# Attention scores of a transformer kernel issued at the pace of the next block's row maxima

## The chip, the cores and the metric

The kernel runs on one core of one Trainium2 chip. The metric is the device time of one execution in microseconds (us). The kernel before took 1959.16 us, the median of 3 runs (1953.23 to 1961.06). The profile comes from one further execution, which took 1958.59 us.

Five engines work side by side, each through its own instruction stream in order: PE (TensorE, matrix products; PEld is its weight load), DVE (VectorE), ACT (ScalarE), POOL (GpSimd) and SP (SyncE), which only issues DMAs here. They wait for one another with semaphores. PE writes to eight PSUM banks of 128 x 512 float32.

## The reference, cut to what matters

One sequence of 2048 tokens with 256 features passes four residual layers: attention with a linear position bias, a layer of 64 experts, attention with low-rank keys and values, and the experts again. The change touches both attention layers, which share one order of work. Per head (16 heads of 16 features), in the first:

```python
scores = jnp.einsum('bhqd,bhkd->bhqk', q, k)
scores = jnp.where(causal[None, None], scores, NEG)
scores = scores + bias[None]
scores = scores / jnp.sqrt(jnp.float32(D))
w = jax.nn.softmax(scores, axis=-1)
ctx = jnp.einsum('bhqk,bhkd->bqhd', w, v).reshape(b, s, e)
return ctx @ Wo + bo
```

The softmax subtracts each query's largest score, so that every score is computed twice: once to find the maxima, and once more, transposed, for the exponents.

## The kernel before

The core of an attention layer (the part between the projections and the experts) is cut into 16 **blocks**: 4 groups of 4 heads, and in each 4 blocks of 512 queries. `BLOCKS` runs through a group's blocks b = 0, 1, 2, 3, and in the last group through 3, 2, 1, 0. A block goes through two passes.

The **maxima** of a block: PE multiplies queries by keys into one of three PSUM banks (L1686; parts on the diagonal get a mask added by small products, L1692), and DVE reduces the bank to row maxima (L2146, L2152). One such product with its reduction is called a maximum here. Block b needs 16b + 10 of them: 10, 26, 42, 58. When the last is reduced, DVE combines them (L2162), PE transposes the result (the **turn**, L1700), DVE splits it in two parts (L2172, L2174), and SP sends them by DMA as extra rows of the query operand. Only then can the block's exponents start.

The **units** of a block: one for each 128 keys, 4(b + 1) of them, each with two scores items (two products each, L1714, on 52 of the rows, into the two `exp_banks`), two exponents on ACT (L1346) and one product of the exponents with the values (L1728, "pv" in the code, called the value product here), which accumulates in one bank over the block. In the last four units of a block the causal mask shortens the rows: 512, 384, 256, 128. After the last value product ACT copies the bank out (L1355), PE transposes it (`ctx`, L1740), and ACT, DVE and POOL finish the context.

While the units of one block run, PE also issues the maxima of the next block. Both share PE's one stream, and the order in it is fixed before the kernel is built: `core_plan()` (L134) keeps four streams, contexts, maxima, scores and value products, and estimated finishing times of the engines. It repeatedly takes the item that can start earliest by those estimates (`ready`), the maxima winning ties over the scores. The turn of a block stands in the maxima's stream behind the first two maxima of the next block (`items.insert(2, ...)`). All engines walk through the same resulting list. `NP` = 3 is the number of buffers for exponents: unit e may not be scored before the value product of unit e - 3.

## Time and profile before

| | us | share of the span |
|---|---|---|
| profiled execution, its own time | 1958.59 | |
| span, first to last instruction | 1956.8 | 100% |
| PE busy | 1677.0 | 86% |
| DVE busy | 1426.4 | 73% |
| ACT busy | 1127.2 | 58% |
| POOL busy | 698.0 | 36% |

The span holds everything but 1.8 us of the execution's time. The two attention cores lie at about 60 to 526 us and 1027 to 1492 us, some 466 us each; the experts fill most of the rest. Busy time adds up what an engine's records cover, so an engine can be busy without being at its peak. PEclk is the TensorE clock that was granted: 1.0 is 2.4 GHz and 0.5 is 1.2 GHz.

### The profile page before, as it was taken

The page shows a single profiled execution, that of the slowest core. Times are in us where ns is not written, and L with a number is a line of the kernel's source. Part 1 is how long each engine was busy: PE and PEld are TensorE (multiplying, and loading weights), DVE is VectorE, ACT ScalarE, POOL GpSimd, SP SyncE. Part 2 cuts the span into 40 slices and gives each one's busy share as a digit, 9 for nine tenths or more (in the row PEclk, how much of TensorE's full clock was granted, in tenths as well). Part 3 has the DMA queues.
Part 4 walks back from the last instruction along what each step waited for, and adds up shares of the span by engine and source line. Part 5 has one row for each costly group of instructions (what it writes and reads, how often), then busy time and mean ns, then how long its engine had stood idle before and what let it go on. Part 6 is the DMA issues. An engine that isn't in the chain of part 4 may idle for free.

```text
span 1956.8 us, 36378 instructions
## 1 busy us (share of the span) xinstructions
PE 1677.0 (86%) x12410; PEld 1037.7 (53%) x12410; DVE 1426.4 (73%) x3057; ACT 1127.2 (58%) x1999; POOL 698.0 (36%) x788
## 2 busy tenths in 40 slices
PE   6899999999977789987788999999999787889910
PEld 5545444445556677775334454544446566777710
DVE  5688888888487765886548788888866788558843
ACT  2155757667557677664233457576664676777610
POOL 6000101000257556545660001010012674754466
PEclk9677989889989999999897779898899899999955
DMA  6540120300075556665854104030003555666643
GB/s 234 174 70 2 30 40 12 57 2 2 23 275 170 178 173 199 203 197 181 250 168 86 20 2 62 6 53 14 2 7 105 217 175 170 204 195 203 202 140 118
DMA packets 127906, 225.96 MB, mean 115 GB/s; under 512 B 15364, under 2 KB 91028, under 8 KB 123444
## 3 DMA queue, kind: packets, MB, share of 16 engines
q1 hardware_dynamic: 103152, 156.49, 26.4%
q0 software_dynamic: 24576, 67.14, 12.7%
q8 instruction: 106, 1.74, 0.4%
q14 instruction: 72, 0.59, 0.1%
HBM read 124.20 MB, written 98.84 MB: 114 GB/s over the span
## 4 chain that ended last, share of the span: by engine, by line
PE 58%; DVE 13%; DMA 9%; issue 8%; POOL 7%; ACT 3%; SPq 1%; DVEq 0%; ACTq 0%; POOLq 0%
PE late_banks L1728 14%; PE late_banks L1686 12%; PE exp_banks L1714 8%; PE late_banks L1517 7%; PE exp_banks L1534 6%; POOL ring_t L1093 4%; DMA ring_t<-token_rows,index_t 3%; DVE chunk_max_t L2146 3%; POOL ring_t L1088 3%; DVE inter_t L2027 3%; PE late_banks L1550 2%; DMA ring_t<-expert_rows,rows_of_t 2%; DMA expert_rows<-outs_t 2%; PE late_banks L1492 2%; PE late_banks L1692 2%
## 5 line engine op out<-in xcount | busy, mean ns | idle before, releaser
L1346 ACT ACTIVATE probs_t<-exp_banks 128x1024 f32<-128x1024 f32 (+3 forms) x640 | 538.9, 896 | 291.7 <-PE exp_banks L1714 289.0
L2146 DVE TENSOR_REDUCE chunk_max_t<-late_banks 128x1 f32<-128x512 f32 (+1 forms) x960 | 602.5, 682 | 111.7 <-PE late_banks L1686 87.4
L1184 POOL TENSOR_SCALAR_AFFINE_SELECT probs_t<-probs_t 128x512 f32<-128x512 f32 x128 | 81.3, 635 | 676.7 <-ACT probs_t L1346 676.7
L1728 PE MATMUL late_banks<-probs_t,values_t 128*32 128x512 f32 (+3 forms) x2560 | 318.7, 572 | 1.9 <-POOL probs_t L1184 1.1
L1093 POOL DMA_INDIRECT ring_t<-expert_rows,rows_of_t x256 | 243.9, 953 | 189.3 <-DVE x_sb_t L2045 127.4
L1517 PE MATMUL late_banks<-tokensT_t,fetched_t 128*128 x2048 | 299.2, 291 | 10.9 <-issue 5.6
L1088 POOL DMA_INDIRECT ring_t<-token_rows,index_t x256 | 251.3, 982 | 139.2 <-PE late_banks L1492 78.5
L2027 DVE TENSOR_TENSOR inter_t<-late_banks,silu_t 64x256 f32<-64x256 f32 x512 | 217.5, 425 | 91.0 <-ACT silu_t L1267 80.0
L1517 PEld LDWEIGHTS late_banks<-tokensT_t,fetched_t 128*128 128x128 f32 x2048 | 255.5, 196 | 41.4 <-issue 22.7
L1686 PE MATMUL late_banks<-contextT_t,Qp_t 50*128 50x512 f32 (+7 forms) x640 | 232.9, 511 | 7.6 <-DVE values_t L2115 2.1
L1534 PE MATMUL exp_banks<-fetched_t,inter_t 64*128 64x128 f32 x2048 | 186.2, 301 | 45.0 <-DVE inter_t L2027 42.6
L1686 PE MATMUL late_banks<-Kp_t,Qp_t 50*128 50x512 f32 (+7 forms) x640 | 213.3, 468 | 2.7 <-DVE chunk_max_t L2146 1.6
L1250 ACT ACTIVATE fetched_t<-weights_t 128x384 f32 x320 | 159.0, 519 | 73.1 <-PE exp_banks L1534 58.5
L2045 DVE SCALAR_TENSOR_TENSOR x_sb_t<-ring_t,row_top_t,x_sb_t 128x256 f32<-128x256 f32 x256 | 122.8, 480 | 98.2 <-DMA ring_t<-expert_rows,rows_of_t 94.2
L1534 PEld LDWEIGHTS exp_banks<-fetched_t,inter_t 64*128 64x128 f32 x2048 | 136.5, 189 | 88.2 <-DVE inter_t L2027 67.1
L1686 PEld LDWEIGHTS late_banks<-contextT_t,Qp_t 50*128 50x128 f32 (+1 forms) x640 | 114.1, 219 | 128.5 <-DVE chunk_max_t L2146 102.8
L1273 ACT ACTIVATE outs_t<-exp_banks 128x512 f32<-128x512 f32 x256 | 150.5, 588 | 42.1 <-DMA expert_rows<-outs_t 23.4
L1686 PEld LDWEIGHTS late_banks<-Kp_t,Qp_t 50*128 50x128 f32 (+1 forms) x640 | 102.8, 202 | 130.0 <-DVE chunk_max_t L2146 104.8
L1714 PE MATMUL exp_banks<-Qp_t,contextT_t 52*128 52x512 f32 (+7 forms) x640 | 148.8, 441 | 12.3 <-DMA Qp_t<-neg_lo_t 8.3
L1714 PE MATMUL exp_banks<-Qp_t,Kp_t 52*128 52x512 f32 (+7 forms) x640 | 142.7, 423 | 6.9 <-ACT probs_t L1346 5.3
L1492 PE MATMUL late_banks<-ident_t,ring_t 128*128 128x128 f32 x512 | 100.3, 291 | 31.6 <-DMA ring_t<-token_rows,index_t 24.7
L2017 DVE COPY fetched_t<-weights_t 128x384 f32 x192 | 81.6, 425 | 60.3 <-PE exp_banks L1534 53.5
(228 smaller groups left out, 1879.5 us busy)
## 6 DMA issues: line engine op xcount, KB each, us to landing
expert_rows<-outs_t SPq DMA_DIRECT2D x256, 256.0 KB
weights_t<-in_experts SPq DMA_DIRECT2D x8, 1728.0 KB, 14.0
Qp_t<-q_rows SPq DMA_DIRECT2D x12, 768.0 KB
weights_t<-in_experts SPq DMA_DIRECT2D x4, 2112.0 KB, 9.7
q_rows<-part_hi_t SPq DMA_DIRECT2D x16, 512.0 KB, 3.2
k_rows<-part_hi_t SPq DMA_DIRECT2D x16, 512.0 KB, 3.9
Kp_t<-k_rows SPq DMA_DIRECT2D x8, 768.0 KB
q_rows<-part_lo_t SPq DMA_DIRECT2D x16, 256.0 KB, 4.3
```

The costliest lines, as they stand in the source:

```text
L1088: pool.indirect_dma_start(ring[:, slot, :], None, token_rows[f][:, :], bass.IndirectOffsetOnAxis(ap=index[h][:, n:n + 1], axis=0))\
L1093: pool.indirect_dma_start(ring[:, slot, :], None, expert_rows[f][h][:, :], bass.IndirectOffsetOnAxis(ap=rows_of[:, t, k:k + 1], axis=0))\
L1250: act.activation(fetched[:, n % NFETCH, blk, :], weights[:, bass.ds(fetches[n][blk], EW)], ACT.Copy)\
L1273: act.activation(outs[:, out % NOUT, :, :].rearrange("p b (s c) -> p s b c", s=2), down_banks(n).rearrange("p s (b c) -> p s b c", b=2), A ...
L1346: act.activation(probs[:, e % NP, 2 * p:2 * p + 2, off:QB], exp_banks[sq % 2][:, :, off:QB], ACT.Exp, scale=D ** -0.5).then_inc(exp_done, 1)
L1517: last = pe.matmul(bank[:, blk * P:(blk + 1) * P], fetched[:, n % NFETCH, blk, k * P:(k + 1) * P], tokensT[:, bass.ds(starts_of[n][blk] + ...
L1534: last = pe.matmul(down_bank(n, side)[:, blk * P:(blk + 1) * P], inter[rows, n % 2, blk * P:(blk + 1) * P], fetched[rows, n % NFETCH, blk, ...
L1686: last = pe.matmul(bank[:, begin:end], Qp[s][rows, p, t * P:(t + 1) * P], Kp[s][rows, p, c * QB:c * QB + end - begin], start=True, stop=c < b)
L1714: last = pe.matmul(exp_banks[sq % 2][:, hh, off:QB], Kp[s][rows, p, j * P:(j + 1) * P], Qp[s][rows, p, b * QB + off:(b + 1) * QB], start=T ...
L1728: last = pe.matmul(pv_banks[n % NPV][32 * h:32 * h + 32, off:QB], values[:, j, GH * g + h, :], probs[:, e % NP, h, off:QB], start=(j == 0) ...
L2027: dve.tensor_tensor(inter[side * EI:(side + 1) * EI, n % 2, :], up, silu[0:EI, n % 2, :], ALU.mult)\
L2146: op = dve.tensor_reduce(chunk_max[:, b, p, chunk_row(r), chunk_col(b, r, c)], bank[:, 0:n].rearrange("q (p k) -> q p k", p=len(parts)), A ...
```

## The change

A scores item of a unit is now ready only when the maxima of the next block have got far enough: with n units of its own block still to be scored, itself included, fewer than `PACE` x n = 5n entries of the maxima's stream may be left before the next block's turn. The last block has no condition.

```diff
+PACE = 5
 ...
+    turn_at = [maxima.index(("turn", g, b)) for g, b in BLOCKS]
 ...
+    def paced(g, b, j):
+
+        after = BLOCKS.index((g, b)) + 1
+        return after == len(BLOCKS) or at[1] > turn_at[after] - PACE * (TPB * (b + 1) - j)
 ...
         if kind == "qk":
             return max(exp_bank_free[scored % 2], turned[item[1:3]]) if item[1:3] in turned and \
-                (item[5] < NP or item[5] - NP in products) else None
+                (item[5] < NP or item[5] - NP in products) and paced(*item[1:4]) else None
```

No instruction is added or removed: 1112 items stand in the list in both kernels. Line numbers of the instructions rise by 7. The order differs in the blocks (0, 0), (0, 1), (0, 2), (1, 2) and (2, 2), and by a few items in (2, 3); from the block (3, 3) on, the two lists are the same but for where they stand in the first items.

The first place is PE's stream in block (0, 1), around its first three value products. `late_banks` are the banks of the maxima and of the value products, `exp_banks` those of the scores, `contextT_t` is the key operand of even groups; `x4` is four rows alike. Before:

```order
L1714 MATMUL exp_banks<-Qp_t,contextT_t 128x512 x2
L1686 MATMUL late_banks<-contextT_t,Qp_t 128x512
L1728 MATMUL late_banks<-probs_t,values_t 32x512 x4
L1686 MATMUL late_banks<-contextT_t,Qp_t 128x512 x2
L1714 MATMUL exp_banks<-Qp_t,contextT_t 128x512 x4
L1686 MATMUL late_banks<-contextT_t,Qp_t 128x512
L1728 MATMUL late_banks<-probs_t,values_t 32x512 x4
L1686 MATMUL late_banks<-contextT_t,Qp_t 128x512 x2
L1714 MATMUL exp_banks<-Qp_t,contextT_t 128x512 x2
L1686 MATMUL late_banks<-contextT_t,Qp_t 128x512
L1714 MATMUL exp_banks<-Qp_t,contextT_t 128x512 x2
L1728 MATMUL late_banks<-probs_t,values_t 32x512 x4
```

In the changed kernel the same block goes on like this:

```order
L1735 MATMUL late_banks<-probs_t,values_t 32x512 x4
L1693 MATMUL late_banks<-contextT_t,Qp_t 128x512 x3
L1721 MATMUL exp_banks<-Qp_t,contextT_t 128x512 x4
L1693 MATMUL late_banks<-contextT_t,Qp_t 128x512
L1735 MATMUL late_banks<-probs_t,values_t 32x512 x4
L1693 MATMUL late_banks<-contextT_t,Qp_t 128x512 x2
L1735 MATMUL late_banks<-probs_t,values_t 32x512 x4
L1693 MATMUL late_banks<-contextT_t,Qp_t 128x512 x2
L1721 MATMUL exp_banks<-Qp_t,contextT_t 128x512 x4
L1693 MATMUL late_banks<-contextT_t,Qp_t 128x512 x4
L1735 MATMUL late_banks<-probs_t,values_t 32x512 x4
```

Between two value products there stood three maxima and one unit's scores; now two to four maxima stand alone in a row, and later in the block seven maxima with the scores of two units alternate with two or three maxima without any.

The second place is PE's stream where block (0, 0) ends and (0, 1) begins, around the turn (`neg_max_t`; `cut_t` is the mask of a diagonal maximum). Before, the 12 rows up to the new block's first value product:

```order
L1692 MATMUL late_banks<-cut_t,ident_t 128x128
L1692 MATMUL late_banks<-cut_t,ident_t 128x64
L1686 MATMUL late_banks<-contextT_t,Qp_t 128x512 x2
L1700 MATMUL late_banks<-ident_t,neg_max_t 16x128
L1686 MATMUL late_banks<-contextT_t,Qp_t 128x512 x6
L1714 MATMUL exp_banks<-Qp_t,contextT_t 128x512 x4
L1686 MATMUL late_banks<-contextT_t,Qp_t 128x512 x2
L1714 MATMUL exp_banks<-Qp_t,contextT_t 128x512 x2
L1686 MATMUL late_banks<-contextT_t,Qp_t 128x512 x2
L1714 MATMUL exp_banks<-Qp_t,contextT_t 128x512 x2
L1686 MATMUL late_banks<-contextT_t,Qp_t 128x512
L1728 MATMUL late_banks<-probs_t,values_t 32x512 x4
```

And now, where the last value product of the old block (32x128) and its context (`sums_t`) stand beside the turn:

```order
L1735 MATMUL late_banks<-probs_t,values_t 32x256 x4
L1693 MATMUL late_banks<-contextT_t,Qp_t 128x512
L1699 MATMUL late_banks<-cut_t,ident_t 128x128
L1699 MATMUL late_banks<-cut_t,ident_t 128x64
L1693 MATMUL late_banks<-contextT_t,Qp_t 128x512
L1735 MATMUL late_banks<-probs_t,values_t 32x128 x4
L1693 MATMUL late_banks<-contextT_t,Qp_t 128x512
L1747 MATMUL late_banks<-ident_t,sums_t 128x128 x4
L1707 MATMUL late_banks<-ident_t,neg_max_t 16x128
L1693 MATMUL late_banks<-contextT_t,Qp_t 128x512 x6
L1721 MATMUL exp_banks<-Qp_t,contextT_t 128x512 x4
```

Before, six maxima stood between the old block's last value product and the turn, too far up for these rows to reach the product. Five of them have moved up between the old block's units, and one is left. At the ends of the blocks (0, 1), (0, 2), (1, 2) and (2, 2) it was 11, 15, 9 and 9 maxima, and is one too. The six behind the turn stay.

## Rows read from the trace of the kernel before

**Rows 1.** The page: busy share of each engine, and the granted clock in 40 slices.
```profile
PE 1677.0 (86%) x12410; PEld 1037.7 (53%) x12410; DVE 1426.4 (73%) x3057; ACT 1127.2 (58%) x1999; POOL 698.0 (36%) x788
...
PEclk9677989889989999999897779898899899999955
```

**Rows 2.** Waits, 60 to 526 us: who waited for whom, us in total, times, longest.
```profile
PEld late_banks L1686 <- DVE chunk_max_t L2146: 105.0, 158, 1.7
...
DVE chunk_max_t L2146 <- PE late_banks L1686: 41.7, 81, 4.5
```

**Rows 3.** Timeline of DVE, units of block (0, 1): start, us, line, count, idle before.
```profile
109.30 1.89 DVE L2146 TENSOR_REDUCE chunk_max_t<-late_banks 128x1 f32<-128x512 f32 x3 [0.49 <-PE late_banks L1686]
111.44 1.89 DVE L2146 TENSOR_REDUCE chunk_max_t<-late_banks 128x1 f32<-128x512 f32 x3 [0.25 <-PE late_banks L1686]
...
116.45 4.28 DVE L2146 TENSOR_REDUCE chunk_max_t<-late_banks 128x1 f32<-128x512 f32 x7 [0.42 <-PE late_banks L1686]
```

**Rows 4.** Timeline of DVE, units of block (0, 2) of the second attention.
```profile
1102.42 1.89 DVE L2146 TENSOR_REDUCE chunk_max_t<-late_banks 128x1 f32<-128x512 f32 x3 [1.90 <-PE late_banks L1686]
1106.28 1.89 DVE L2146 TENSOR_REDUCE chunk_max_t<-late_banks 128x1 f32<-128x512 f32 x3 [1.98 <-PE late_banks L1686]
```

**Rows 5.** Busy time by stretch: us, then busy us of each engine, clock, DMA.
```profile
core 0: us, PE busy (x) PEld busy (x) DVE busy (x) ACT busy (x) POOL busy (x), PEclk, DMA share, GB/s
107.80:112.00 4.20, 4.20 (x31) 1.62 (x30) 3.46 (x6) 3.75 (x5) 0.00 (x0) 1.00 1.02 140
187.20:193.50 6.30, 6.30 (x61) 3.68 (x53) 5.82 (x10) 5.93 (x7) 0.00 (x0) 1.00 0.01 3
...
120.70:131.20 10.50, 10.17 (x51) 5.56 (x46) 9.97 (x21) 0.50 (x2) 0.62 (x1) 0.68 0.22 40
124.40:132.10 7.70, 6.76 (x18) 3.10 (x17) 7.63 (x16) 0.00 (x0) 0.62 (x1) 0.50 0.05 17
75.00:104.20 29.20, 27.39 (x130) 14.63 (x130) 19.18 (x34) 9.30 (x14) 3.17 (x5) 0.50 0.17 50
```

**Rows 6.** The same, from a block's first scores to the clock's rise.
```profile
1060.60:1066.50 5.90, 5.63 (x23) 2.37 (x23) 3.43 (x6) 3.87 (x4) 0.00 (x0) 0.50 0.82 142
276.80:288.20 11.40, 11.32 (x47) 4.77 (x47) 7.09 (x14) 6.26 (x7) 0.00 (x0) 0.50 0.01 3
424.20:431.60 7.40, 7.09 (x27) 3.26 (x27) 4.30 (x8) 4.52 (x5) 0.00 (x0) 0.50 0.01 2
1091.90:1110.90 19.00, 18.74 (x73) 7.51 (x73) 9.98 (x17) 10.00 (x11) 0.00 (x0) 0.50 0.00 1
```

**Rows 7.** Timeline of PE, block (1, 2)'s last value product to (1, 3)'s first.
```profile
265.60 0.43 PE L1728 MATMUL late_banks<-probs_t,values_t 128*32 128x128 f32 x8
...
276.77 1.22 PE L1714 MATMUL exp_banks<-Qp_t,Kp_t 52*128 52x512 f32 x4
...
280.53 1.93 PE L1728 MATMUL late_banks<-probs_t,values_t 128*32 128x512 f32 x8
```

**Rows 8.** Timeline, block (2, 3)'s last value product to (3, 3)'s first.
```profile
418.27 0.42 PE L1728 MATMUL late_banks<-probs_t,values_t 128*32 128x128 f32 x8
...
419.97 0.27 PE L1700 MATMUL late_banks<-ident_t,neg_max_t 128*16 128x128 f32 x1
...
420.68 0.28 DVE L2174 TENSOR_TENSOR neg_lo_t<-late_banks,neg_hi_t 16x128 fp32r<-16x128 f32 x1
...
424.24 1.22 PE L1714 MATMUL exp_banks<-Qp_t,Kp_t 52*128 52x512 f32 x4 [0.35 <-DMA Qp_t<-neg_lo_t]
...
427.82 1.93 PE L1728 MATMUL late_banks<-probs_t,values_t 128*32 128x512 f32 x8
```

**Rows 9.** Timeline of PE, two value products with seven maxima between them.
```profile
189.16 1.06 PE L1728 MATMUL late_banks<-probs_t,values_t 128*32 128x512 f32 x8
...
193.94 0.64 PE L1728 MATMUL late_banks<-probs_t,values_t 128*32 128x512 f32 x4
```

## The prediction, made before the changed kernel was run

> **What bounds the kernel now.** I read the page first: PE is busy 86% of the span, DVE 73%, ACT 58%, and the granted clock is often below its top digit in slices that lie in the attention cores [rows 1]. That an engine is called busy does not say that it sets the pace, so I went to the waits of the first core. Its longest wait on the shared path is PE's weight load for a maximum, kept back by DVE's reduction of an earlier one: 105.0 us in 158 waits. The other way round, DVE waited for the same products 41.7 us in 81 waits [rows 2]. PE and DVE thus alternate over three banks, and it has to be read stretch by stretch which of them is late.
>
> At the full clock it is DVE. In block (0, 1) it starts a run of three maxima at 109.30 and the next at 111.44, so a unit takes 2.14 us; a long run of seven takes 4.28 us, or (4.28 - 0.68) / 6 = 0.60 us from start to start, with 0.68 for the last one [rows 3]. Three make 1.80 us, and 0.33 us are lost at each value product. At the half clock it is PE: the same three maxima and one unit take 1106.28 - 1102.42 = 3.86 us, with DVE idle for 1.98 of them [rows 4]. So 1 us of such a mixture at the half clock costs 1 - 2.14/3.86 = 0.45 us.
>
> The stretches show when the clock is lost. While units and maxima are mixed, it is 1.00; between the last value product of a block and the next block's first scores, where only maxima are left, ACT has 0.50 us of work in 10.5 us, the clock is 0.68 on average and then 0.50 [rows 5]. PE's records cover 10.17 of those 10.50 us, so its busy share is no guide here. In that stretch the half clock costs nearly nothing, since DVE is busy 7.63 of 7.70 us [rows 5]. The price comes behind it: the new block starts at 0.50 and stays there for 5.9 to 19.0 us after its first scores, of which four cases stand in [rows 6].
>
> **The change, part by part.** It adds and removes no instruction. It moves units later, so that the maxima which stood alone at a block's end now lie between its units. As the maxima are DVE's work and 58 of them take at least 58 x 0.60 = 34.8 us against 12 units x 2.14 = 25.7 us, DVE bounds a block as a whole at the full clock either way, and the first-order gain is nothing: filling ACT's idle time at a block's end buys nothing that DVE doesn't allow. What is left are four smaller terms.
>
> *First, the loss at the value products.* Where paced, two units with ten maxima are ordered as product, three maxima, product, two maxima, scores, four maxima, scores, one maximum. Before, these cost two mixed units and four lone maxima: 2 x 2.14 + 4 x 0.60 = 6.68 us. The floor is DVE's 10 x 0.60 = 6.0 us. The nearest row is a stretch of seven maxima with four scores items between two value products, 193.94 - 189.16 = 4.78 us [rows 9], that is 0.58 over 4.20; with three lone maxima behind the other product at 1.80 to 2.14 us the pair would take 6.58 to 6.92. Those seven maxima were diagonal ones with mask products, which burden PE, so I lean to the floor and take 6.45, a gain of 0.2 us. The long form stands 10 times in each layer, so 20 pairs: -4 us, with bounds of -13.6 (floor) and +4.8 (6.92).
>
> *Second, the block's end.* From the last value product to the next block's first took 280.53 - 265.60 = 14.93 us with 19 maxima [rows 7]. The form that the change makes at ten places already stands once in each layer, at the end of (2, 3): 427.82 - 418.27 = 9.55 us with 11 maxima [rows 8]. Eight maxima fewer are 4.8 us, so 14.93 would have become 10.13, and the short form is 0.6 us better at its best. It began with the clock still full, though: its last value product took 0.42 us [rows 8], and 0.50 is granted from 424.20 on [rows 6]. In the changed kernel the last units of a block have short rows (384, 256, 128) and are stretched over some 20 maxima. PE's work there is thin, and I expect the clock to fall up to 10 us earlier. The maxima and short products at the half clock cost something between nothing (DVE hides it) and the 0.6 gained plus 0.45 us for each of some 3 us. I take a net +0.2 us a place, +2 us in all, between -6 and +8.
>
> *Third, block (0, 0) of the first attention.* It runs wholly at 0.50: in 29.2 us DVE is busy 19.18 us [rows 5], since four units at PE's pace come first and lone maxima at DVE's pace after. Here pacing does overlap the two. Before, a pair of two units and four lone maxima costs 2 x 3.86 + 2.4 = 10.1 us; the same ten maxima with PE as the bound cost at least 7.7 us (extra maxima free) and at most 10.1. These units are the diagonal ones with shorter rows, and there are two pairs; half of the difference on both is 2.4 us, and one maximum more before the first scores, where DVE has nothing to do until 75 us, adds 0.6. I take -3 us, between 0 and -6. In the second attention the mixed units brought the clock back within that block; thinner work may not, so I take 0.
>
> *Fourth, the recovery.* The turn's result needs from 420.68 to 424.24, 3.6 us, by DVE, SP and the DMA, before the first scores [rows 8]. That is not shortened, and the one example of the new form lost the clock anyway and got it back 7.4 us after its first scores [rows 6, 8], in the middle of the 5.9 to 19.0 of the old form. I count 0. Blocks (0, 1) and (0, 2) have four full units or fewer before pacing thins them, so a late rise is likelier there; that is a part of the rival below.
>
> The DMAs of the turns keep their order on SP. POOL's masks and ACT's exponents follow the units and have idle time: ACT waits for nothing but scores. Later exponents free nothing that anyone else waits for, since the units from block (3, 3) on stand where they stood.
>
> Sum: -4 + 2 - 3 + 0 = -5 us against the profiled execution's 1958.59 us, or 1953.6. That execution is 0.6 us below the median of 1959.16, so I say **1954 us**.
>
> The Trainium skill, "TensorE: Matmul & The Clock Gate", section "A second HAM failure mode: psum-queue depth-cycling", says that a matmul stream which pauses briefly and often because it cycles through PSUM banks can make the clock swing between its two levels. This kernel cycles through three banks throughout and its mixed stretches stay at 1.00, which disagrees as long as units come every 2.14 us; whether it holds at one unit in 3.3 us no row shows. By that rule the second rival would come true, by the trace of before the forecast.
>
> **Rivals.** *The clock stays up (faster).* With a shorter stretch of lone maxima, the clock might survive some of the ten ends. Each recovery of 7 to 11 us at the half clock would give back 0.45 x 9 = 4 us; five of ten give -20, so about 1934 us. For it speaks that PE's thin stretch shrinks from 15 to 10 us; against it that the short form lost the clock in both layers at (2, 3), and that the units before it were denser than they will be now. Chance 0.15.
>
> *The clock falls inside the paced units (slower).* Place: the full-width units of (0, 1), (0, 2), (1, 2) and (2, 2), about 15 in each layer. There PE gets one unit and five maxima in 3.3 us in place of one unit and three in 2.14. If the clock falls, PE becomes the bound: the pace is 3.86 us with the two added maxima free and 3.86 + 1.20 = 5.06 with none hidden; at 4.5 a unit loses 1.2 us. All 30 would cost 36 us, half of them 18, which beside the forecast's -5 makes 1972 us. It decides from about 9 units on, where the 5 us are used up. For it: lone maxima do lose the clock. Against it: the stretch from 187.20 to 193.50, with ten diagonal maxima within it, kept 1.00 [rows 5]. Chance 0.13.
>
> *The new order changes nothing that can be told (the first-order argument alone).* The gain at value products fails and block (0, 0) gives its 3 us, which the ends take back: 1958 us. Chance 0.17.
>
> That the change does nothing at all is excluded by the order of instructions.
>
> **Chances and range.** Forecast 0.55, with an own range of 1947 to 1960; the clock stays 0.15; the clock falls 0.13; nothing 0.17. A measurement of this kernel can tell 0.5%, 9.8 us, from no change, so faster means below 1949.4 and slower above 1969.0. Faster: 0.15 and a fifth of the forecast's 0.55, 0.26. Slower: two thirds of the rival's 0.13, and 0.01, so 0.10. Same: 0.64. The range reaches into both clock cases: 1940 to 1970.
>
> **What the changed profile would show.** Runs of DVE's maxima with idle time of 0.1 to 0.2 us behind value products in place of 0.25 to 0.33: the first term. About 9.6 to 10.4 us from the last value product of a block to the first of the next: the second. The first block at 0.50 reaching the value product that stood at 104.2 us about 3 us sooner: the third. The granted clock at 1.00 through the full-width paced units of (0, 2) and (1, 2), falling at the narrow ones or behind, and rising 6 to 11 us after the first scores: the forecast. 0.50 in the middle of the paced units with DVE idle for over 1 us a unit: the slower rival. A clock of 1.00 across a block's end: the faster one. The prediction is wrong if the attention cores, 466 us each, change by more than 5 us each.

## The result

| | time, median (lowest to highest) |
|---|---|
| before | 1954.85 us (1953.23 to 1961.06, 5 runs) |
| changed | 1971.42 us (1969.65 to 1979.01, 5 runs) |
| ratio | 1.0071, 95% interval 1.0039 to 1.0104 |

The change makes the kernel slower by 0.7%. Forecast were 1954 us and a range of 1940 to 1970; the median lies outside it, and where the second rival stood (the clock falls inside the paced units, 1972 us, chance 0.13). The ratios with an interval, here and below, are those on record, for which an execution over 1.5% above the fastest of its kernel counts as slow; none of these ten does. The profiled execution of the changed kernel took 1969.65 us with a span of 1967.9, 11.1 over the one before. Between the first value product of block (0, 0) and that of (3, 3), the first attention took 344.9 us in place of 348.9, and the second 360.4 in place of 349.5. The order of work is the same in both, so the first gained and the second lost.

The page of the changed kernel, the same two lines as in [rows 1]:

```profile
PE 1690.8 (86%) x12410; PEld 1042.9 (53%) x12410; DVE 1427.1 (73%) x3057; ACT 1127.5 (57%) x1999; POOL 694.1 (35%) x788
...
PEclk9788989899989999998885789698899898999965
```

DVE, ACT and the counts of instructions are as before; PE is busy 13.8 us more for the same 12410 products. So the products' records are longer; there are not more of them.

Waits of the changed kernel, 60 to 522 us of the span (who waited for whom, us, times, longest), answering to [rows 2]:

```profile
PEld late_banks L1693 <- DVE chunk_max_t L2153: 113.5, 168, 1.7
DVE chunk_max_t L2153 <- PE late_banks L1693: 46.1, 77, 5.4
```

The two still alternate; nothing new is waited for. In the changed kernel all lines lie 7 further down: L1735 are value products, L1721 scores, L1693 maxima's products, L2153 and L2159 DVE's reductions.

**Where the clock stays, the order does what the forecast said, and a little more.** DVE in block (1, 2) of the first attention (start, us, line, count, idle before):

```profile
250.17 3.79 DVE L2153 TENSOR_REDUCE chunk_max_t<-late_banks 128x1 f32<-128x512 f32 x6 [0.24 <-PE late_banks L1693]
254.19 6.07 DVE L2153 TENSOR_REDUCE chunk_max_t<-late_banks 128x1 f32<-128x512 f32 x10 [0.24 <-PE late_banks L1693]
260.62 1.89 DVE L2153 TENSOR_REDUCE chunk_max_t<-late_banks 128x1 f32<-128x512 f32 x3 [0.36 <-PE late_banks L1693]
```

Ten maxima in a row take 260.62 - 254.19 = 6.43 us with one loss of 0.36 behind them; the forecast had 6.45 for the pair of units, and 6.68 before. PE's value products of the same block, and the first of the next block (start, us, line, shape, count), answering to [rows 7]:

```profile
254.44 1.06 PE L1735 MATMUL late_banks<-probs_t,values_t 128*32 128x512 f32 x8
259.10 1.07 PE L1735 MATMUL late_banks<-probs_t,values_t 128*32 128x512 f32 x8
261.11 0.85 PE L1735 MATMUL late_banks<-probs_t,values_t 128*32 128x384 f32 x8
265.79 0.64 PE L1735 MATMUL late_banks<-probs_t,values_t 128*32 128x256 f32 x8
267.23 0.42 PE L1735 MATMUL late_banks<-probs_t,values_t 128*32 128x128 f32 x8
276.33 1.93 PE L1735 MATMUL late_banks<-probs_t,values_t 128*32 128x512 f32 x8
```

The long stretch (seven maxima) takes 259.10 - 254.44 = 4.66 us, the short one 2.01, and the block's end 276.33 - 267.23 = 9.10 us in place of 14.93 [rows 7], 1.0 less than the 10.13 that eight maxima fewer account for.

**In the second attention the same block loses the clock.** The same view there (`x8` are the products of one unit; the long stretch lies between the first two rows):

```profile
1228.47 1.07 PE L1735 MATMUL late_banks<-probs_t,values_t 128*32 128x512 f32 x8
1233.14 1.94 PE L1735 MATMUL late_banks<-probs_t,values_t 128*32 128x512 f32 x8
1236.77 1.51 PE L1735 MATMUL late_banks<-probs_t,values_t 128*32 128x384 f32 x8
1243.37 1.08 PE L1735 MATMUL late_banks<-probs_t,values_t 128*32 128x256 f32 x8
1245.64 0.65 PE L1735 MATMUL late_banks<-probs_t,values_t 128*32 128x128 f32 x8
1256.47 1.93 PE L1735 MATMUL late_banks<-probs_t,values_t 128*32 128x512 f32 x8
```

At 1228.47 eight value products take 1.07 us, at 1233.14 they take 1.94: the clock fell from 2.4 to 1.2 GHz at the end of a long stretch that itself still took 4.67 us (the trace has the fall at 1233.18). From there the short stretch takes 3.63 us, the next long one 6.60 in place of 4.68, and the end 10.83 in place of 9.10. Busy time by stretch of the changed kernel (us, busy us of each engine, granted clock, DMA): the long stretch at either clock, the 12 us before the fall, the stretches behind this fall and behind that of block (0, 1), and the half clock at the start of the second core:

```profile
core 0: us, PE busy (x) PEld busy (x) DVE busy (x) ACT busy (x) POOL busy (x), PEclk, DMA share, GB/s
254.44:259.10 4.66, 4.29 (x25) 2.03 (x25) 4.66 (x9) 2.40 (x3) 0.64 (x1) 1.00 0.03 11
1236.77:1243.37 6.60, 6.60 (x51) 4.81 (x49) 4.49 (x8) 1.31 (x3) 0.63 (x1) 0.50 0.00 1
1221.00:1233.00 12.00, 11.70 (x77) 4.67 (x69) 11.27 (x19) 8.30 (x10) 0.63 (x1) 1.00 0.50 76
1233.20:1245.60 12.40, 12.40 (x87) 7.45 (x87) 7.57 (x13) 2.73 (x6) 1.90 (x3) 0.50 0.00 1
1076.20:1093.60 17.40, 17.40 (x105) 9.72 (x97) 11.45 (x19) 5.20 (x8) 2.54 (x4) 0.50 0.49 72
1028.40:1069.30 40.90, 39.25 (x177) 20.92 (x178) 30.10 (x54) 11.42 (x15) 3.16 (x5) 0.50 0.23 63
```

The reader is to see who is full. At the full clock it is DVE (4.66 of 4.66 us), at the half clock PE (6.60 of 6.60) with DVE idle a third of the time. And the clock doesn't come back: in the 12.4 and 17.4 us behind a fall PE has no gap at all in its records, yet 0.50 stays. At the start of the second core it stays 40.9 us, through all of block (0, 0). In the first profile of the kernel before it was back while (0, 0) ran, but two later profiles of the kernel before show that block wholly at 0.50 too.

The whole block (1, 2) with its end, before (first and second attention), then changed (the same two), shows gain and loss in one row each:

```profile
242.47:280.53 38.06, 37.40 (x279) 19.41 (x279) 33.33 (x58) 21.84 (x27) 3.78 (x6) 0.88 0.37 58
1209.62:1247.78 38.16, 37.60 (x280) 19.65 (x279) 33.37 (x58) 21.84 (x27) 3.78 (x6) 0.86 0.39 58
```

```profile
239.56:276.33 36.77, 35.12 (x279) 17.73 (x278) 33.14 (x58) 21.63 (x27) 3.78 (x6) 0.97 0.39 61
1213.58:1256.47 42.89, 42.45 (x280) 23.14 (x279) 33.42 (x58) 21.63 (x27) 3.78 (x6) 0.73 0.32 50
```

Before, 38.1 us at a mean clock of 0.88 or 0.86, all of the half clock lying behind the last value product, where it is hidden behind DVE. Changed, 36.8 us if the clock stays among the units, 42.9 if it falls there. A gain of 1.3 against a loss of 4.8.

### The profile page after: what moved, and what is told of

Read it like the earlier page. It is cut to its first block, busy times and chain, and to the rows that moved or that the text cites. A ratio compares the mean times of both kernels' runs of the same rounds, so it can differ in the third digit from the quotient of the medians.

```text
span 1967.9 us, 36378 instructions
## 1 busy us (share of the span) xinstructions
PE 1690.8 (86%) x12410; PEld 1042.9 (53%) x12410; DVE 1427.1 (73%) x3057; ACT 1127.5 (57%) x1999; POOL 694.1 (35%) x788
## 3 DMA queue, kind: packets, MB, share of 16 engines
q0 software_dynamic: 24576, 67.14, 12.6%
## 4 chain that ended last, share of the span: by engine, by line
PE 57%; DVE 14%; DMA 10%; issue 7%; POOL 7%; ACT 3%; SPq 1%; DVEq 0%; ACTq 0%; POOLq 0%
PE late_banks L1735 14%; PE late_banks L1693 12%; PE exp_banks L1721 8%; PE late_banks L1524 6%; PE exp_banks L1541 6%; POOL ring_t L1100 4%; DVE chunk_max_t L2153 3%; DMA ring_t<-token_rows,index_t 3%; DVE inter_t L2034 3%; DMA ring_t<-expert_rows,rows_of_t 3%; POOL ring_t L1095 2%; DMA expert_rows<-outs_t 2%; PE late_banks L1557 2%; PE late_banks L1499 2%; PE late_banks L1699 2%
## 5 line engine op out<-in xcount | busy, mean ns | idle before, releaser
L2153 DVE TENSOR_REDUCE chunk_max_t<-late_banks 128x1 f32<-128x512 f32 (+1 forms) x960 | 602.3, 683 | 115.3 <-PE late_banks L1693 91.0
L1735 PE MATMUL late_banks<-probs_t,values_t 128*32 128x512 f32 (+3 forms) x2560 | 326.0, 584 | 2.6 <-POOL probs_t L1191 1.1
L1693 PE MATMUL late_banks<-contextT_t,Qp_t 50*128 50x512 f32 (+7 forms) x640 | 233.5, 502 | 10.0 <-DVE chunk_max_t L2153 2.7
L1693 PE MATMUL late_banks<-Kp_t,Qp_t 48*128 48x512 f32 (+7 forms) x640 | 214.3, 467 | 3.4 <-DVE chunk_max_t L2153 2.4
L1693 PEld LDWEIGHTS late_banks<-contextT_t,Qp_t 50*128 50x128 f32 (+1 forms) x640 | 111.7, 214 | 143.5 <-DVE chunk_max_t L2153 120.7
L1693 PEld LDWEIGHTS late_banks<-Kp_t,Qp_t 50*128 50x128 f32 (+1 forms) x640 | 102.2, 200 | 136.3 <-DVE chunk_max_t L2153 109.0
L1721 PE MATMUL exp_banks<-Qp_t,contextT_t 52*128 52x512 f32 (+7 forms) x640 | 153.2, 446 | 8.9 <-DMA Qp_t<-neg_lo_t 6.6
L1721 PE MATMUL exp_banks<-Qp_t,Kp_t 52*128 52x512 f32 (+7 forms) x640 | 142.7, 424 | 7.4 <-ACT probs_t L1353 5.8
## 6 DMA issues: line engine op xcount, KB each, us to landing
weights_t<-in_experts SPq DMA_DIRECT2D x8, 1728.0 KB, 13.8
```

The costliest lines, as they stand in the source:

```text
L1693: last = pe.matmul(bank[:, begin:end], Qp[s][rows, p, t * P:(t + 1) * P], Kp[s][rows, p, c * QB:c * QB + end - begin], start=True, stop=c < b)
L1721: last = pe.matmul(exp_banks[sq % 2][:, hh, off:QB], Kp[s][rows, p, j * P:(j + 1) * P], Qp[s][rows, p, b * QB + off:(b + 1) * QB], start=T ...
L1735: last = pe.matmul(pv_banks[n % NPV][32 * h:32 * h + 32, off:QB], values[:, j, GH * g + h, :], probs[:, e % NP, h, off:QB], start=(j == 0) ...
L2153: op = dve.tensor_reduce(chunk_max[:, b, p, chunk_row(r), chunk_col(b, r, c)], bank[:, 0:n].rearrange("q (p k) -> q p k", p=len(parts)), A ...
```

## Experiments

Theory A: the clock falls inside the long stretch (seven maxima between value products) and the thin mixture doesn't bring it back. Theory B: the late units cost by their order itself, whatever the clock. Theory C, formed after the first eight runs: the order gains some us, and half-clock time *among units* costs more than that; half-clock time in lone maxima is free. The runs were made on three chips, and each kernel is compared with the kernel before on its own chip. On the first of them the kernel before takes about 1960 us, on the other two 2044 to 2050; the added time lies outside the attention cores. Ratios of different chips are set beside each other with care only. "Among units" is the time at 0.50 from the first to the last value product of each block, summed over the blocks up to (2, 3) of a layer; the half clock at the ends is the rest, from a block's last value product to the next block's first; "core" is the time from the first value product of (0, 0) to that of (3, 3).

**Evened stretches (first chip).** The pairs are reordered into five and five maxima. In words, not code:

```diff
-  product, 3 maxima, product, 2 maxima, scores, 4 maxima, scores, 1 maximum, product
+  product, 2 maxima, scores, 3 maxima, product, 2 maxima, scores, 3 maxima, product
```

> The changed kernel, with each pair of paced units ordered anew: in place of three maxima, value product, seven maxima with the scores of both units, value product, now twice: two maxima, one unit's scores, three maxima, value product. Units stay as late as in the changed kernel; only the stretch of seven maxima without a value product is gone. Theory A (the clock falls inside that stretch and the thinned mixture does not bring it back before the block's end): no fall inside the full-width paced units, the second attention core loses its 10 us, and the time is 8 to 16 us under the changed kernel's 1971, near 1957. Theory B (late units cost by themselves, whatever the clock: the next block's start finds less finished work): 1968 to 1975, like the changed kernel.

1968.12 us against 1959.65, ratio 1.0031 [1.0010, 1.0052]: theory B's number, and not the 1957 of theory A. Half clock among units was 50.4 and 30.9 us in the two layers; the changed kernel's layers have 35 to 71. The interval overlaps that of the changed kernel, so a gain over it is not shown. The test is weaker than it looks, in two ways. The edit reaches eight of the ten long stretches of a layer; one in (0, 1) and one in (0, 2) stay, and the one fall among the units that lasted (3.4 us) lies in the former. And the evened order lost the gain by itself: the block (1, 2) with its end took 38.6 and 39.1 us with at most 0.1 us of half clock among its units, where the changed kernel takes 36.8 so and the kernel before 38.1.

**The kernel before with its block ends filled (first chip).** Two products of scores, which nobody reads, into the first of the `exp_banks` behind each lone maximum:

```diff
+                        if item in lone:
+                            filler(s, b)
```

> The kernel before, with a filler of two scores products that nobody reads, into the idle exp_banks, behind each maximum that stands where no unit is under way (at the blocks' ends). PE gets work there that costs DVE nothing. If the clock at the blocks' ends is lost because PE's work is thin there, and its price is 0.45 us for each us of mixed work at the half clock behind it (5.9 to 19.0 us a block, ten blocks that change places, two more at (2, 3)), the clock stays at 1.00 across most ends and the time falls by 20 to 45 us, to 1910 to 1935. If the fall has another cause (a fixed rhythm, the DMA of the turn), the clock still falls there and the time stays within 5 us of 1955.

1957.52 us against 1959.65, ratio 0.9994 [0.9966, 1.0022]. So the 20 to 45 us that I expected if the clock held at the ends didn't come, though it held there for the most part. Blocks (1, 2) and (1, 3), with their ends:

```profile
241.44:279.26 37.82, 36.34 (x309) 19.41 (x309) 33.11 (x58) 21.36 (x27) 3.78 (x6) 1.00 0.36 58
279.26:317.00 37.74, 37.64 (x290) 16.87 (x292) 32.68 (x56) 29.28 (x35) 3.18 (x5) 0.95 0.01 2
```

Block (1, 2) ran at 1.00 throughout, and was 0.2 to 0.3 us shorter than at 0.86 to 0.88. Over the core, half clock at the ends fell from 69 and 61 us to 10 and 21, and the core from 349 to 346 and 348. So half clock behind the last unit is nearly free, as [rows 5] had said. The half clock among the units stayed, 30.0 and 30.6 us for 30.3 and 32.7: here, too, the clock was often down when a block's first units ran, in block (1, 3) from 279.4 us on, after an end at the full clock. Filled ends alone don't take it away.

**Both kernels once more, with a profile (first chip).**

> The kernel before once more, for a second profile. Theory A: the clock falls only at the blocks' ends, as in the first profile (no fall between two value products of full width). The recoveries behind the blocks' first scores vary between 6 and 19 us as before. Time 1953 to 1961.

> The changed kernel once more, for a second profile. Theory A: the clock falls inside paced units at some places and not at others, and not at the same ones as in the first profile ((0, 1) and (1, 2) of the second core, (0, 0) never back), because the thin stretches are of marginal density. Where it falls, a pair of paced units takes 10 us and not 6.7. Theory B: the same places and the same losses whatever the clock.

1970.66 us for before and 1952.36 for the changed kernel: the other way round. Single executions scatter by about 10 us each way (23 runs of before on this chip: 1953.26 to 1972.13), so from here on I compared many timed executions and, from the profiles, single blocks. In the kernel before no fall began among the units of a block, in the changed kernel one did that lasted, in (0, 1) of the first attention.

**The changed kernel on the second chip, and its parts.** The edits are cut to their one line each. All of it; only the blocks (0, 2), (1, 2) and (2, 2); only group 0:

```diff
-        return after == len(BLOCKS) or at[1] > turn_at[after] - PACE * (TPB * (b + 1) - j)
+        return b != 2 or g == G - 1 or at[1] > turn_at[after] - PACE * (TPB * (b + 1) - j)
...
+        return g > 0 or at[1] > turn_at[after] - PACE * (TPB * (b + 1) - j)
```

> The changed kernel, timed on the same chip as the next three. All theories: 8 to 16 us over the kernel before's runs of this call. Theory A, refined by the profiles so far (the half clock costs about 0.4 us for each us in which units run, and nothing in the stretch of lone maxima): the profile's attention cores sum up as about 331 us from first value product to that of block (3, 3), plus 0.42 times the half-clock time among units, 30 to 75 us of it.

> Pacing applied only to the blocks (0, 2), (1, 2) and (2, 2), of twelve units; (0, 0) and (0, 1) stand as in the kernel before. Theory A: the loss sits in (0, 0) and (0, 1), which start at the half clock and are thinned before it is back; without them each of the three blocks in each layer saves 1 to 1.5 us where the clock holds and loses 5 where it falls (one time in four), so 0 to 6 us under the kernel before. Theory B (late units cost in themselves): three of five places are left, so 4 to 10 us over the kernel before.

> Pacing applied only to group 0, that is (0, 0), (0, 1) and (0, 2). Theory A: most of the changed kernel's loss is here, 6 to 14 us over the kernel before; the profile shows (0, 1)'s units in 21 to 27 us, 27 where the clock is not back within its first three units. Theory B: three of five places, 4 to 10 us over it, and no link between a block's time and the clock.

Ratios 1.0070 [1.0032, 1.0108], 0.9985 [0.9951, 1.0019] and 1.0001 [0.9974, 1.0028]. The loss shows on this chip too, but in the longest executions. Five of the changed kernel's twelve took 2074.86 us or more and four of those with only (0, 2), (1, 2) and (2, 2) paced 2069.93 or more; of 35 of before none took more than 2059.01. Over all twelve the mean times are 1.0067, 1.0042 and 1.0012 of before's; without those nine the first two would be 1.0017 and 0.9999, so 0.9985 is no evidence that pacing three of the five blocks costs nothing. The five ran at a mean clock of 0.866 to 0.871, under all 35 of before (0.876 to 0.888), so they look like what theory C is about and not like noise.

For group 0 alone theory A had 6 to 14 us and theory B 4 to 10; its median is 0.1 us over before. For the other part the mean, 1.0042, is what theory B says for three of five places. So these ratios don't decide between the theories. The blocks do. Of the block (1, 2) in the six layers of these three kernels: 36.8 and 36.8 us with the clock kept, 42.9 and 42.9 with a fall, and 38.1 and 38.0 where it wasn't paced. The same instructions in the same order take 6.1 us more when the clock falls among them, and 1.3 less than before when it doesn't; a price of the order by itself would be there in both. What I had expected of the core, 331 us and 0.42 for each us among units, gives 349.9 and 354.3 us for the changed kernel's two layers here; measured were 349.2 and 354.6 (45.1 and 55.4 us among units).

**Scores issued three times (second chip).** In each stretch of seven maxima and two units' scores (13 a layer) the first scores of the second unit are repeated, to make PE's work denser without touching the order:

```diff
+                        for hh in range(2) if item in held else ():
+                            for _ in range(2):
+                                pe.matmul(exp_banks[sq % 2][:, hh, :], ...)
```

> The changed kernel, with the first scores products of the second unit in every stretch of seven maxima issued three times (into the same bank, before the real ones), which makes PE's work there denser by two pairs of products. Theory A: no fall inside the full-width paced units, earlier rises in (0, 1), half-clock time among units back at 30 to 40 us a layer, and the time 5 to 12 us under the changed kernel, less up to 4 for PE's added work. Theory B: more work on PE, so the changed kernel's time plus 0 to 8 us.

Ratio 1.0049 [1.0026, 1.0072], with 44.4 and 46.1 us among units, where theory A had 30 to 40. That is within what the changed kernel shows, so the half clock was hardly reduced, and the time fits theory B as well. The run is inconclusive.

**Maxima's products issued twice (third chip).** Every maximum in a run of three or more among a block's units, then those at the ends as well. The pages count 107 and 185 more products a layer, since some maxima have two:

```diff
+                            if item in twice:
+                                pe.matmul(bank[:, begin:end], ..., start=True, stop=True)
                             last = pe.matmul(bank[:, begin:end], ..., start=True, stop=c < b)
```

> The changed kernel with the product of every maximum that stands among the units of a block in a run of three or more (85 products a layer) issued twice into the same bank; DVE's work and all orders are kept. Theory C (the loss is half clock that arises among the units, because PE's work is thin there): the added load, for which PE has some 1.3 us of room in each pair of units at the full clock, keeps the clock or brings it back; the half clock among units falls from about 50 us a layer to 30 or less, the attention core ends 8 us or more sooner a layer than in the changed kernel, and the ratio to before is 0.990 to 1.000. Theory B (the late units cost by their order, whatever the clock): the ratio stays 1.005 or more with the half clock gone. If the load is too little to hold the clock, it must cost instead: PE bounds at the half clock, 0.42 us for each doubled product there, ratio 1.010 or more with 50 us of half clock or more.

> As the run before, and the products of the lone maxima behind a block's last unit doubled as well (136 a layer). Theory C: the half clock at the block ends, about 40 us a layer, mostly goes too, and with it the slow first units of the next block; the ratio is 0.985 to 0.998, 2 us or more a layer under the run before. If half clock in lone maxima costs nothing and is not inherited, the ratio equals that of the run before within 0.002. Theory B: 1.005 or more.

Ratios 1.0042 [1.0016, 1.0068] and 1.0035 [1.0011, 1.0059]: my number, 0.990 to 1.000, missed, and so did the 30 us or less of half clock among units (34.2 and 52.6, then 34.3 and 43.0). The two ratios are equal within 0.002, as expected for the case that half clock in lone maxima costs nothing and isn't handed on. Blocks (1, 2) in both layers and (0, 2) of the first, in the first of the two kernels:

```profile
247.12:285.14 38.02, 37.60 (x297) 19.93 (x296) 33.28 (x58) 21.83 (x27) 3.78 (x6) 0.94 0.38 59
1264.42:1301.90 37.48, 36.05 (x297) 19.04 (x297) 33.53 (x59) 21.63 (x27) 3.78 (x6) 0.99 0.40 60
...
132.07:179.78 47.71, 46.95 (x315) 24.12 (x313) 37.11 (x64) 21.88 (x27) 3.16 (x5) 0.82 0.00 1
```

In the eight blocks (1, 2) and (2, 2) of these two kernels the clock never fell among the units, against 3 of 16 in all profiles of the changed kernel. But the doubled products cost about 1 us in such a block (37.4 to 38.1 for 36.8 in (1, 2)), and where the clock is down anyway, as in (0, 2), 47.7 us against 41.8 to 44.5 usually. No net gain is left. That the load holds the clock is suggested, not shown: at 3 in 16, eight without a fall would come by chance 2 times in 10.

**Pacing only (1, 2) and (2, 2), and the changed kernel with its ends filled (third chip).** The edit of the first; that of the second is the filler shown above, in the changed kernel:

```diff
+        return g == 0 or after == len(BLOCKS) or at[1] > turn_at[after] - PACE * (TPB * (b + 1) - j)
```

> The changed kernel with pacing only in the blocks (1, 2) and (2, 2), the complement of the run that paced group 0 alone (ratio 1.0001). Blocks (0, 0) to (0, 2) as before. Theory C: the long blocks reach their paced stretches at the full clock and lose it rarely; half clock among units stays near 33 to 40 us a layer, ratio 0.998 to 1.002; the core is 1 to 2 us a layer shorter at equal half clock. Theory B: the two blocks have half of the paced units, so half of the loss, 1.0035.

> The changed kernel with two further products of scores behind each lone maximum at a block's end (into a bank whose scores are already used up), as was done to the kernel before (ratio 0.9994 there). Theory C in the form that the clock falls among the paced units themselves: half clock in the gaps falls below 15 us a layer, that among units stays at 40 us or more, and the ratio stays 1.003 to 1.008. In the form that the half clock is inherited from the block's end and only not made good in the thin first units: that among units falls to 30 or less and the ratio to 0.995 to 1.000.

Ratio of the first 1.0041 [1.0011, 1.0071], with 55.5 and 70.9 us among units: for theory C I had expected 33 to 40 and 0.998 to 1.002, and 1.0035 for theory B, which is nearer. The profiled execution is the longest of the twelve. It showed the first fall inside (2, 2):

```profile
1371.45:1413.40 41.95, 40.85 (x241) 19.74 (x241) 33.15 (x57) 21.65 (x27) 3.78 (x6) 0.73 0.36 53
```

41.95 us with its end for 37.0 to 37.6 in all eight layers of the changed kernel. A fall came in (1, 2) of the first layer as well (42.9 us), while the two blocks took 36.8 and 37.1 us where it didn't. So the falls among their units are again where these blocks lose; the rest of the half clock lay in unpaced blocks. These two blocks are also two of the three paced in the run above with 0.9985 (1.0042 over all twelve), so the parts can't be added up more finely than some 0.3%.

The filled ends gave 0.9996 [0.9961, 1.0031]; over all twelve executions the mean is 1.0024 of before's. The changed kernel unfilled wasn't timed on this chip (1.0070 on the second). Blocks (1, 2) and (1, 3) of the first attention, and (2, 2) of the second:

```profile
243.10:280.28 37.18, 35.78 (x301) 18.75 (x300) 33.16 (x58) 21.34 (x27) 3.79 (x6) 1.00 0.37 60
280.28:317.00 36.72, 36.61 (x294) 16.47 (x292) 32.83 (x57) 29.62 (x36) 3.19 (x5) 1.00 0.01 2
1353.69:1397.14 43.45, 42.81 (x264) 22.25 (x263) 33.30 (x57) 21.65 (x27) 3.79 (x6) 0.73 0.35 51
```

Half clock at the ends went to 5 and 25 us; among the units it was 26 and 55, so the expectation's first form holds in one layer and its second in the other. Where nothing is handed on and nothing falls, the blocks (1, 2) and (1, 3) with their ends take 37.2 and 36.2 us (the second row runs 0.5 us past the block's end at 316.49), but the clock still falls inside a paced stretch, as in (2, 2). The ratio suggests that filling takes back part of what the change cost, or all of it; across chips and with these intervals that is not shown, and nothing is gained over before.

**Pacing only where the profiles showed a gain, and two more profiles (second chip).** Blocks (0, 0), (0, 2) and (2, 2), without and with filled ends. Theory C' is theory C with the blocks' gains and losses independent of each other:

```diff
-        return after == len(BLOCKS) or at[1] > turn_at[after] - PACE * (TPB * (b + 1) - j)
+        return (g, b) not in ((0, 0), (0, 2), (2, 2)) or at[1] > turn_at[after] - PACE * (TPB * (b + 1) - j)
```

> The changed kernel with pacing only in the blocks (0, 0), (0, 2) and (2, 2). Over the profiles so far (two executions of before, three of the changed kernel, two layers each) these blocks with their ends took 2.9, 1.7 and 1.3 us less than before, while (0, 1) and (1, 2) took 2.3 and 1.0 more. Theory C' (each paced stretch gains about 1.3 us where the clock stays and loses 4 to 6 where it falls, and what it leaves behind decides the next block): about -6 us a layer if the blocks are independent, ratio 0.994 to 0.998. Rival (the place of the fall only moves: the clock that was not lost in one block is lost in the next): ratio 0.998 to 1.003, with (0, 1) or (0, 3) longer.

> The same three blocks paced, and the two further products of scores behind each lone maximum at the blocks' ends (filling alone: ratio 0.9994 on before, 0.9996 on the changed kernel, where it took away the loss of 0.7%). Theory C': less half clock is handed to the next block, 0.990 to 0.997. Rival: what filling gives is the same as what avoiding the bad blocks gives, so no sum: 0.998 to 1.001.

Ratios 1.0029 [0.9998, 1.0061] and 1.0022 [0.9987, 1.0056]. The profiled cores were 344.3 and 348.1, then 337.7 and 347.4 us, below at least five of the six of before, but the timed medians aren't below: a block's gain in a few profiles doesn't show in twelve executions. The first ratio lies in the rival's range, with (0, 3) longer (41.4 and 41.3 us for 38.8), the second just over it, and neither in that of theory C'. No version that I ran beats the kernel before.

> The kernel before, once more with a profile: its first value product of (0, 0) to that of (3, 3) took 349 to 352 us in four layers so far, with 30 to 37 us of half clock among units. Theory C': again 348 to 352 and 28 to 38. If the loss of the changed kernel is chance of the executions that were profiled, before shows a layer above 355 too.

> The changed kernel, once more with a profile: 345 to 360 us in six layers so far, with 35 to 71 us of half clock among units. Theory C': mean of the two layers above 350, half clock among units above 40, and each block (1, 2) either 36.8 us with its end (no fall) or 42.9 (a fall within the paced stretch).

Before: cores of 343.4 and 351.7 us with 21.1 and 35.9 among units; one of each lies below what I expected, and none above. Changed: 357.4 and 354.6 with 59.7 and 55.4, as expected. In the latter the clock fell in (0, 2), which no layer had shown so far (with its end 51.4 us). In (1, 2) it fell 0.4 us before the last value product in one layer, with 38.7 us between my two expected values, and 12.6 us before it in the other:

```profile
134.33:185.74 51.41, 50.24 (x285) 25.74 (x283) 37.26 (x64) 21.70 (x27) 3.17 (x5) 0.67 0.01 1
251.19:289.87 38.68, 38.21 (x280) 20.75 (x279) 33.34 (x58) 21.65 (x27) 3.79 (x6) 0.85 0.36 58
1262.76:1305.62 42.86, 42.40 (x280) 23.14 (x279) 33.42 (x58) 21.63 (x27) 3.79 (x6) 0.73 0.36 53
```

The means over all profiled executions, three of before (six layers) and four of the changed kernel (eight), each block with its end, in us; in brackets the half clock among its units:

| block | before | changed |
|---|---|---|
| (0, 0) | 23.7 (8.1) | 21.0 (8.6) |
| (0, 1) | 32.4 (4.4) | 34.2 (10.6) |
| (0, 2) | 43.9 (5.5) | 44.0 (7.0) |
| (0, 3) | 38.8 (6.0) | 39.8 (8.4) |
| (1, 2) | 38.1 (0.0) | 39.5 (4.8) |
| (1, 3) | 37.8 (3.8) | 38.5 (5.5) |
| (2, 2) | 38.4 (0.0) | 37.1 (0.0) |
| (2, 3) | 44.1 (3.9) | 46.4 (6.7) |
| core | 349.3 (31.8) | 352.6 (51.6) |

The four short blocks (1, 0), (1, 1), (2, 0), (2, 1), left out of the rows, are equal within 0.1 us. At the ends there were 64.4 us of half clock before and 41.2 in the changed kernel, so the sum is nearly the same (96.2 and 92.8 us): it has moved among the units.

**Where the half clock among the units begins.** In the six layers of before it is all handed on: the clock was down when the block's first value product ran, and no fall began among the units. In the changed kernel 7.6 of the added 19.8 us are more of that, and 12.2 us come from falls that begin among the units. In all profiles together there are 32 blocks (1, 2) or (2, 2) paced as in the changed kernel, with filled ends or not, and 24 unpaced ones. Seven of the 32 have such a fall with over 0.4 us of half clock behind it, none of the 24 has any; so many on one side would come by chance about 1.5 times in 100. In all seven the fall stands in the last 0.21 us of the block's first stretch of seven maxima, or within 0.04 us behind it, 12 to 13 us before the last value product. In (0, 1), paced from its second unit on, falls began within either of its two such stretches in six of eight layers. So theory A names the place rightly, and theory C the price.

Across the eight layers of the changed kernel the core's time rises by 0.43 us for each us of half clock among units (six of before: 0.54); that is near the price 0.45 worked out from [rows 3, 4]. By my estimate from these figures 19.8 us more of it cost 8.5 us a layer, and the difference of 3.3 leaves 5.2 us that the order gained.

## Why the prediction was wrong

**What bounds the kernel** held: DVE at the full clock, PE at the half clock, 0.45 us for each us of half clock in mixed work and nearly nothing in lone maxima (0.3 us in a block).

**First term** (loss at value products, 0.2 us a pair): right at the full clock, 6.43 us measured for 6.45. **Second term** (the block's end, +0.2 a place): mis-sized both ways. It foresaw the clock falling up to 10 us earlier and charged some 3 us of half clock for it. Where the clock stays among the units, nothing of this comes: in (1, 2) it fell only 7 us behind the last value product, and (1, 2) and (2, 2) gained 1.3 us each, where the first two terms together were to bring 0.2 a place. Where it falls among them, it does so 12 to 13 us before the last value product, and (1, 2) takes 42.9 us for 38.1, a loss of 4.8. **Third term** (block (0, 0), -3 us, in the first attention alone): 25.3 us became 22.4 in layers that ran wholly at the half clock, so -2.9; the mean over both layers is -2.7 each. But the block doesn't always run so: in three of four profiles of the changed kernel the clock came back within it in the first attention (18.4 to 18.8 us), and in one of three of before. In the second attention the clock came back within (0, 0) in one of three executions of before and in none of four changed; of that I had written "I take 0".

**The step that failed is the price of the clock**: in the second term the early fall, and above all the fourth, the recovery: "I count 0", with the remark that the late rise in thin blocks was "a part of the rival". Together they stood for +2 us; by the estimate above the half clock cost 8.5 us a layer, 17 in both. The blocks that follow or hold the thin mixture spend 6.2 us (0, 1), 1.5 (0, 2), 2.4 (0, 3), 4.8 (1, 2), 1.7 (1, 3) and 2.8 (2, 3) more at half clock among their units than before. Of the 19.8 us, 7.6 are handed on, which is the fourth term, and 12.2 fall anew among the units. I had taken only lone maxima for work that loses the clock. The paced mixture loses it now and then too, and seldom brings it back: of the seven falls among the units of (1, 2) and (2, 2) in all profiles none was over before the block's end; in (0, 1) some were over after 3.4 us. Before, the units came packed and lone maxima came packed, so the half clock lay where it is free; the change spread PE's work evenly and moved the half clock under the units.

**The rival** gave the right mechanism, and its number by luck. It foretold falls in half of 30 full-width units at 1.2 us each. The falls come at the end of a block's full-width units, and slow the short ones behind them. Inside (1, 2) they came in 3 of 8 layers, in (2, 2) in none of 8 (once each in two of the experiments); the rest of the half clock that began among units is falls in (0, 1) and one in (0, 2), and 7.6 us a layer are handed on to next blocks, the unpaced ones too. Its remark that it decides from about 9 units on was a slip: at 1.2 us a unit, 5 us are used up by about four. My evidence against it, the stretch from 187.20 to 193.50 at 1.00 [rows 5], was one stretch of ten diagonal maxima with mask products, 61 products in 6.3 us; the paced one before the fall has 77 in 12.0. "PE busy" is nearly the same in both (6.30 of 6.30, 11.70 of 12.00), the number of products in a microsecond is not (9.7 and 6.4).

The Trainium skill, "TensorE: Matmul & The Clock Gate", section "A second HAM failure mode: psum-queue depth-cycling", pointed to this outcome, as the prediction says: it ties a swinging clock to a matmul stream that pauses briefly and often as it cycles through PSUM banks. The clock does fall here in such a stream (113.5 us in 168 waits, longest 1.7). But the kernel before waits for the same banks nearly as often (105.0 us in 158 waits), and among the units of (1, 2) and (2, 2) its clock stays at 1.00 in all six layers. What differs between the two is the mixture of units and maxima.

**What stays open.** That the half clock among the units costs the time is shown by blocks of equal instructions with and without a fall. That the thinner mixture brings the falls rests on the count of 7 in 32 against 0 in 24; the three experiments made for it (evened stretches, tripled scores, doubled maxima) didn't take the loss away. The cores of the profiled executions differ by 2 x 3.3 = 6.6 us on average, the timed medians by 10 to 17. The profiled executions of the changed kernel lie among its shortest: 1969.65 us is the lowest of five, 2043.05 the lowest of twelve (median 2060.41). Of before one does too: 2028.64 us lies under all 23 timed beside it. In the result's own pair the two cores make 6.9 of the 11.1 us between the spans, and the rest lies outside, where both kernels run the same order. Whether the rest is the choice of executions, or lies between the cores, isn't settled. Nor is why the same order falls in (1, 2) and hardly in (2, 2).

## What to carry to other kernels

Where two engines alternate and the clock of one can fall, ask where its half-clock time lies, not how much there is: where another engine sets the pace it was nearly free here, and spreading the same work moved it under the units that it slows (31.8 to 51.6 us a layer, with the sum at the ends and among the units nearly unchanged). An edit whose first-order gain is nothing (the bound engine's work is unchanged) has only such second-order terms, and here they lost. When single executions scatter by more than the effect, compare blocks by cases (clock kept, clock lost) and count the cases, in all profiles at hand. And count the longest executions too: they may be the effect.

## What the runs showed of the hardware

- The granted clock fell to 0.50 while PE's records left 0.3 us of 12.0 free, and stayed there for 12.4, 17.4 and 40.9 us with PE busy 12.40, 17.40 and 39.25 us. PE's busy share didn't tell here where the clock falls or rises.
- Executions of one kernel differ by the places of their falls: cores of 345 to 360 us in eight layers of the changed kernel. Whole times of before were 1953 to 1972 us over 23 executions on one chip.
- Nearly the same mean clock can go with quite different times. On the second chip twelve executions of the changed kernel had a mean clock of 0.878 and 35 of before 0.882, with 13.8 us between their mean times; on the third, filled ends had 0.897 for 0.881 of before, with 4.9 us over it.
- One block of equal instructions, (1, 2) of the changed kernel, took 36.8 us with the full clock among its units and 42.9 with a fall 12.5 us before its last value product.
- Half clock in lone maxima cost about 0.3 us in a block of 38 (37.82 at 1.00, with the fillers, for 38.06 at 0.88).
